# Attention kernel: the value matmuls of a step issued in one piece after the first couple of heads

## The chip, the cores and the metric

The kernel runs on one core of a Trainium2 chip. The metric is the device time of one execution in microseconds (us); lower is better. Its engines are named as in the profile: PE (TensorE matmuls), PEld (TensorE weight loads), DVE (VectorE), ACT (ScalarE), POOL (GpSimd), SP (SyncE, which issues the DMAs here).

## What is computed

The reference is one pre-norm transformer layer on x of shape (4, 2048, 256): x + attention(layernorm(x)), then + FFN(layernorm(x)). The attention is what matters here: 16 heads of width 16, rotary positions, causal, softmax in float32.

```
scores = einsum('bhqd,bhkd->bhqk', Q, K) / sqrt(16)
scores = where(causal_mask, -inf, scores)
attn = softmax(scores);  out = einsum('bhqk,bhkd->bhqd', attn, V)
x = x + einsum('bsd,ed->bse', out, Wo)
x = x + relu(layernorm(x) @ w1 + b1) @ w2 + b2
```

## The kernel before, in words

Three stages follow each other: `stage1` (layernorm, projections, rotation), `stage2` (attention, the largest) and `stage3` (output projection and FFN). The change touches `stage2` alone.

`stage2` runs 16 iterations, one for each batch entry and group of four heads (G = 4). An iteration has 40 steps (`STEPS`, NS = 40). A step is a pair (c, kb): c is one of four chunks of 512 queries, kb a block of 128 keys. A chunk c has 4c full steps (kb under 4c), then four diagonal steps, whose scores are 512, 384, 256 and 128 columns wide. An iteration thus has 24 full and 16 diagonal steps.

Two computations are interleaved:

- Scores, exponentials and values of step s. `score_tile` (L829) makes, for each head j = 0 to 3, a tile of 128 keys by up to 512 queries in PSUM. The four tiles of a step go round three banks (`SB = 3`, `s_bank`), and a tile waits (`p_done`, `read_before`) until ACT has read the tile three before it in the order of all tiles. ACT takes the exponential of each tile (L960) into `prob`, of which there are three buffers; POOL zeroes the triangle in diagonal steps (L990). `pv_step` (L848) multiplies the values with `prob` of step s - 2 (`BEHIND` = 2), for four heads on four strips of 32 columns of the array, accumulating in one bank (`O_BANK`) over the chunk. It is issued in two parts, each with half of the columns of all four heads. Only part 0 waits (for `p_done` or `mask_done`, and at a chunk's start for `o_copied`); part 1 counts `pv_done`, for which ACT waits before it writes a `prob` buffer again and before it copies the finished chunk (L951).
- Row maxima, 20 steps ahead (`LAG`). `max_pair` (L191, with small masking matmuls at L196 in couple 0 of diagonal tiles) makes query-by-key scores of a couple of heads into two banks. There are four such banks: couple 0 (heads 0/1) has two, couple 1 (heads 2/3) the other two. Before each matmul PE waits (`m_read`) until DVE has read what was in its bank. DVE takes the maximum of a couple with one reduce (L208), except that couple 1 of a diagonal tile takes two masked operations (L215), each of which waits for one matmul only. After a chunk's last tile three small DVE operations (L907, L912, L917) pass the maxima on.

The order on PE is written out by hand in `iteration` of `stage2`'s tensor block. In all steps that have maxima it is, for each couple: score, max, score, max, then a half of the value step:

```
for pair in range(NP):
    score_tile(i, p, s, 2 * pair)
    max_pair(nc, pe, ops, ps, t, pair, (1,))
    score_tile(i, p, s, 2 * pair + 1)
    max_pair(nc, pe, ops, ps, t, pair, (0,))
    value_step(i, p, s, pair)
```

The last 20 steps of the last iteration have no maxima (t reaches `STEPS_M`). They take another order, with two value parts, and the last two value steps are called after the loop, also with two parts. PE carries out its queue in order: a matmul that waits holds all behind it. On DVE and ACT it is the same.

Of the kernel before, what the change touches and what calls it, by code (L numbers as in the profile page):

```python
# [28 lines left out]
CH = 512  # L29
NC = S // CH  # L30
TPC = CH // P
# [19 lines left out]
NS = len(STEPS)  # L51
# [11 lines left out]
def is_diagonal(s):  # L63
    c, kb = STEPS[s]
    return kb >= TPC * c


def diagonals(s):

    return sum(is_diagonal(t) for t in range(s))  # L70
# [91 lines left out]
def m_use(t, j):  # L162

    return G * t + j
# [15 lines left out]
def max_pair(nc, pe, ops, ps, t, pair, heads=(1, 0)):  # L180

    p, use = t // NS % 2, m_use(t, 2 * pair)
    if pair == 0 and t % NS == 0:
        pe.wait_ge(ops.m_in[p], 128 * (t // NS // 2 + 1))
    qt, kc = MAX_TILES[t % NS]
    w = min(CH, (qt + 1) * P - kc * CH)
    for jj in heads:
        rows = slice(HROWS * jj, HROWS * (jj + 1))
        pe.wait_ge(ops.m_read, use + 2 - jj)
        masked = masked_on_pe(pair, qt, kc)  # L190
        last = nc.tensor.matmul(ps[:, bank_of(use + jj), 0:w], ops.mq[rows, p, pair, qt * P:(qt + 1) * P],  # L191
                                ops.mk[rows, p, pair, kc * CH:kc * CH + w], start=True, stop=not masked)
        for part in range(2 if masked else 0):

            n = P - HROWS * part
            last = nc.tensor.matmul(ps[:, bank_of(use + jj), w - n:w], ops.pick[rows, part], ops.upper[rows, part, 0:n],  # L196
                                    start=False, stop=part == 1)
        last.then_inc(ops.m_ready, 1)
# [456 lines left out]
def stage2(nc, x, qk_d, v_d, att_d, rows_d, rinv_d, weight_ds, weights, ops):  # L655
    with ExitStack() as ctx:
# [6 lines left out]
        part, m_ready, m_read = ops.part, ops.m_ready, ops.m_read  # L663
# [31 lines left out]
        BEHIND = NPROB - 1  # L695
# [9 lines left out]
        def s_bank(s, j):  # L705

            return S_BANK + (G * s + j) % SB

        def read_before(i, s, j):

            u = G * s + j
            last_in_bank = u - SB if u >= SB else max(t for t in range(ST) if t % SB == u) - ST
            return ST * i + last_in_bank + 1

        def prob_of(i, s):
            return prob[:, (NS * i + s) % NPROB]
# [96 lines left out]
        @block.tensor  # L813
        def _(pe):
            def filler_pair(p, s, pair):

                qt, kc = MAX_TILES[(s + LAG) % NS]
                for jj in range(2):
                    rows = slice(HROWS * jj, HROWS * (jj + 1))
                    nc.tensor.matmul(ps[:, M_BANK + 2 * pair + jj], mq[rows, p, pair, qt * P:(qt + 1) * P],  # L820
                                     mk[rows, p, pair, 0:CH], start=True, stop=True)

            def score_tile(i, p, s, j):

                c, kb = STEPS[s]
                q0 = max(0, kb - TPC * c) * P
                pe.wait_ge(p_done, G + read_before(i, s, j))
                rows = slice(HROWS * (j % 2), HROWS * (j % 2 + 1))
                nc.tensor.matmul(ps[:, s_bank(s, j), q0:CH], ak[rows, p, j // 2, kb * P:(kb + 1) * P],  # L829
                                 aq[rows, p, j // 2, c * CH + q0:(c + 1) * CH], start=True, stop=True  # L830
                                 ).then_inc(s_ready, 1)

            def pv_step(i, p, s, part):

                c, kb = STEPS[s]
                q0 = max(0, kb - TPC * c) * P
                half = (CH - q0) // 2
                if part == 0:
                    if kb == 0:
                        pe.wait_ge(o_copied, NC * i + c)  # L840
                    if is_diagonal(s):
                        pe.wait_ge(mask_done, G * (NDIAG * i + diagonals(s) + 1))
                    else:
                        pe.wait_ge(p_done, ST * i + G * s + G + G)
                cols = slice(q0 + half * part, q0 + half * (part + 1))
                for j in range(G):

                    last = nc.tensor.matmul(ps[32 * j:32 * j + 32, O_BANK, cols], v[:, p, kb, j, :],  # L848
                                            prob_of(i, s)[:, j, cols], start=kb == 0 and part == 0,
                                            stop=kb == TPC * (c + 1) - 1 and part == 1)  # L850
                if part == 1:
                    last.then_inc(pv_done, 1)

            def value_step(i, p, s, part):

                if s >= BEHIND:
                    pv_step(i, p, s - BEHIND, part)
                elif i > 0:
                    pv_step(i - 1, 1 - p, NS + s - BEHIND, part)

            def iteration(i, p, use):

                pe.wait_ge(a_in[p], A_DMAS * 16 * (use + 1))
                pe.wait_ge(v_in[p], 16 * (use + 1))
                for s in range(NS):
                    t = NS * i + s + LAG
                    if t == STEPS_M:
                        pe.wait_ge(m_read, NM + m_use(STEPS_M, 0))
                    if s in CHUNK_START:
                        pe.wait_ge(rows_in[STEPS[s][0]], 16 * ROWS_DMAS * (i + 1))  # L870
                    if t < STEPS_M:


                        for pair in range(NP):
                            score_tile(i, p, s, 2 * pair)
                            max_pair(nc, pe, ops, ps, t, pair, (1,))
                            score_tile(i, p, s, 2 * pair + 1)
                            max_pair(nc, pe, ops, ps, t, pair, (0,))
                            value_step(i, p, s, pair)
                        continue  # L880
                    score_tile(i, p, s, 0)
                    score_tile(i, p, s, 1)
                    if is_diagonal(s):
                        filler_pair(p, s, 0)
                    score_tile(i, p, s, 2)
                    value_step(i, p, s, 0)
                    score_tile(i, p, s, 3)
                    if is_diagonal(s):
                        filler_pair(p, s, 1)
                    value_step(i, p, s, 1)  # L890

            for t in range(EARLY, LAG):
                for pair in range(NP):
                    max_pair(nc, pe, ops, ps, t, pair)
            for u in range(NIT // 2):
                iteration(2 * u, 0, u)
                iteration(2 * u + 1, 1, u)
            for s in range(NS - BEHIND, NS):
                for part in range(2):
                    pv_step(NIT - 1, 1, s, part)  # L900
# [478 lines left out]
```

## Time and profile before

| | |
|---|---|
| median of 2 runs | 2064.44 us (2060.8 to 2068.07) |
| the profiled execution | 2068.45 us |
| its span | 2066.7 us |
| busy in the span: PE, DVE, ACT, POOL | 1958.2, 1835.6, 1515.4, 627.5 us |
| steps with scores and maxima | from 240 to 1589 us |

The profile's rows come from one execution. Times of a timeline are counted from the span's start; in its rows the first number is the start, the second the time to the end of the last of the instructions that the row merges. A PE matmul's end is modelled, and consecutive matmuls overlap, so PE's busy share says little of how full it is. For the same reason a DVE reduce or an ACT operation is reported a little longer than the distance at which the next one can start.

### The profile page before, as it was taken

The numbers are of one execution on the slowest core, as the hardware profiler recorded it, in microseconds if no ns is written. First come the engines' busy times: TensorE is split into PE (matmuls) and PEld (weight loads), VectorE is DVE, ScalarE is ACT, GpSimd is POOL, SyncE is SP. The second block draws the span as 40 slices with busy tenths as digits, with TensorE's granted clock in tenths as the row PEclk, the third lists the DMA queues.
The fourth block names the chain that finished last, engine by engine and source line by source line (L and its number), as shares of the span: only waits on it lengthen the run. The fifth ranks groups of instructions, "written<-read, shape, count | busy, mean of one in ns | idle before, by whom it ended". The sixth has DMA issues, their size and how long they took to land. (4 is left out here: it accounts for less than half of the span.)

```text
span 2066.7 us, 54533 instructions
## 1 busy us (share of the span) xinstructions
PE 1958.2 (95%) x20128; PEld 821.6 (40%) x20128; DVE 1835.6 (89%) x3190; ACT 1515.4 (73%) x3253; POOL 627.5 (30%) x1252
## 2 busy tenths in 40 slices
PE   6887799999999999999999999999999889999998
PEld 3444133232333333333333333333333156777776
DVE  7999999999999999999999999999997057777775
ACT  6995298887899888988889888898888623333332
POOL 8998022324221222212222122221212223333331
PEclk9998599999999999999999999999999689999999
DMA  5666533030312304123041230412301112222220
GB/s 206 229 241 216 113 74 69 18 70 18 80 38 55 70 18 80 37 56 70 18 80 36 57 69 19 80 34 58 69 8 35 55 64 86 86 85 81 84 84 26
DMA packets 133607, 153.49 MB, mean 74 GB/s; under 512 B 23936, under 2 KB 99712, under 8 KB 133120
## 3 DMA queue, kind: packets, MB, share of 16 engines
q1 hardware_dynamic: 133376, 150.46, 28.2%
q8 instruction: 140, 2.29, 0.5%
q14 instruction: 91, 0.75, 0.1%
HBM read 90.64 MB, written 59.77 MB: 73 GB/s over the span
## 5 line engine op out<-in xcount | busy, mean ns | idle before, releaser
L960 ACT ACTIVATE s_prob<-s_ps 128x512 f32<-128x512 f32 (+3 forms) x2560 | 1200.1, 536 | 159.8 <-PE s_ps L829 131.6
L208 DVE TENSOR_REDUCE part_max<-s_ps 128x2 f32<-128x1024 f32 (+3 forms) x1024 | 1082.7, 1117 | 13.6 <-PE s_ps L191 8.0
L829 PE MATMUL s_ps<-aq,ak 64*128 64x512 f16 (+3 forms) x2560 | 764.9, 355 | 4.4 <-ACT s_prob L960 1.7
L848 PE MATMUL s_ps<-s_prob,s_v 128*32 128x256 f32 (+3 forms) x10240 | 745.3, 363 | 0.0
L191 PE MATMUL s_ps<-mk,mq 64*128 64x512 f16 (+3 forms) x2560 | 654.0, 358 | 43.0 <-DVE part_max L208 34.9
L990 POOL TENSOR_SCALAR_AFFINE_SELECT s_prob<-s_prob 128x128 f32<-128x128 f32 x1024 | 292.1, 294 | 1105.6 <-ACT s_prob L960 1093.5
L829 PEld LDWEIGHTS s_ps<-aq,ak 64*128 64x128 f16 x2560 | 196.5, 94 | 478.2 <-ACT s_prob L960 413.2
L848 PEld LDWEIGHTS s_ps<-s_prob,s_v 128*32 128x32 f32 x10240 | 202.7, 108 | 392.1 <-issue 229.4
L215 DVE CUSTOM_DVE_ANT_0 s_ps<-s_ps,mask_sb 128x512 f32<-128x512 f32 (+3 forms) x512 | 241.4, 510 | 17.4 <-PE s_ps L191 16.9
L191 PEld LDWEIGHTS s_ps<-mk,mq 64*128 64x128 f16 x2560 | 156.5, 93 | 117.9 <-DVE part_max L208 98.5
L1263 ACT ACTIVATE s_h_f<-s_ps,s_b_s 128x512 f32<-128x512 f32 x128 | 88.0, 687 | 107.0 <-PE s_ps L1128 86.0
L1138 PE MATMUL s_ps<-w_hi,s_h_hi 128*128 128x256 f16 x512 | 139.6, 273 | 2.0 <-DVE s_h_lo L1203 2.0
L1138 PE MATMUL s_ps<-w_lo,s_h_hi 128*128 128x256 f16 x512 | 139.6, 273 | 0.0
L1138 PE MATMUL s_ps<-w_hi,s_h_lo 128*128 128x256 f16 x512 | 139.6, 273 | 0.0
L1203 DVE TENSOR_TENSOR s_h_lo<-s_h_f,s_h_hi 128x512 f16<-128x512 f32 x128 | 99.9, 781 | 4.4
L142 POOL TENSOR_TENSOR o_in<-o_in,r_in 128x1024 f32<-128x1024 f32 x16 | 37.8, 2365 | 189.5 <-DMA r_in<-rinv_scratch 189.5
L1201 DVE CAST s_h_hi<-s_h_f 128x512 f16<-128x512 f32 x128 | 61.8, 483 | 31.3 <-ACT s_h_f L1263 26.2
L196 PE MATMUL s_ps<-upper_sb,pick_sb 64*128 64x128 bf16 (+1 forms) x1024 | 89.1, 206 | 0.0
L1257 ACT CAST s_xt_hi<-s_ps 128x512 f16<-128x512 f32 x32 | 17.2, 589 | 89.8 <-PE s_ps L1118 89.8
L1128 PE MATMUL s_ps<-s_xt_hi,w_hi 128*128 128x512 f16 x256 | 77.4, 384 | 2.7 <-DVE s_xt_lo L1196 2.6
L1128 PE MATMUL s_ps<-s_xt_lo,w_hi 128*128 128x512 f16 x256 | 77.1, 383 | 0.0
L1128 PE MATMUL s_ps<-s_xt_hi,w_lo 128*128 128x512 f16 x256 | 77.1, 383 | 0.0
(103 smaller groups left out, 1772.9 us busy)
## 6 DMA issues: line engine op xcount, KB each, us to landing
v_scratch<-s_vst SPq DMA_DIRECT2D x32, 512.0 KB, 3.7
s_v<-v_scratch SPq DMA_DIRECT2D x16, 1024.0 KB, 12.2
att_scratch<-s_o SPq DMA_DIRECT2D x64, 256.0 KB, 2.5
aq<-qk_scratch SPq DMA_DIRECT2D x96, 128.0 KB, 4.4
ak<-qk_scratch SPq DMA_DIRECT2D x96, 128.0 KB, 7.2
s_xin<-x SPq DMA_DIRECT2D x16, 512.0 KB, 4.2
qk_scratch<-s_r_lo SPq DMA_DIRECT2D x64, 128.0 KB, 1.9
qk_scratch<-s_r_hi SPq DMA_DIRECT2D x64, 128.0 KB, 2.0
```

The source lines that it names most:

```text
L191: last = nc.tensor.matmul(ps[:, bank_of(use + jj), 0:w], ops.mq[rows, p, pair, qt * P:(qt + 1) * P], ops.mk[rows, p, pair, kc * CH:kc * CH ...
L196: last = nc.tensor.matmul(ps[:, bank_of(use + jj), w - n:w], ops.pick[rows, part], ops.upper[rows, part, 0:n], start=False, stop=part == 1)
L208: nc.vector.tensor_reduce(ops.part[:, qt // TPC, :, pair, qt % TPC, kc], ps[:, bank_of(use):bank_of(use) + 2, 0:w], AX.X, ALU.max).then_in ...
L215: nc.vector.tensor_tensor_reduce(out=ps[:, bank, 0:w], in0=ps[:, bank, 0:w], in1=ops.mask[:, CH - w:CH], scale=1.0, scalar=MASKED, op0=ALU ...
L829: nc.tensor.matmul(ps[:, s_bank(s, j), q0:CH], ak[rows, p, j // 2, kb * P:(kb + 1) * P], aq[rows, p, j // 2, c * CH + q0:(c + 1) * CH], st ...
L848: last = nc.tensor.matmul(ps[32 * j:32 * j + 32, O_BANK, cols], v[:, p, kb, j, :], prob_of(i, s)[:, j, cols], start=kb == 0 and part == 0, ...
L960: nc.scalar.activation(prob_of(i, s)[:, j, q0:CH], ps[:, s_bank(s, j), q0:CH], ACT.Exp, scale=1.0 / (SQK * DK ** 0.5)).then_inc(p_done, 1)
L990: nc.gpsimd.affine_select(out=block, in_=block, compare_op=ALU.is_ge, fill=0.0, base=0, pattern=[[1, P]], channel_multiplier=-1).then_inc( ...
L1128: last = nc.tensor.matmul(ps[:, H_BANK + f % 2], w[:, k, f * P:(f + 1) * P], a[:, p, k], start=q == 0, stop=q == len(mm) - 1)
L1138: last = nc.tensor.matmul(ps[:, Y_BANK + pair, t * D:(t + 1) * D], a[:, p, k, tt * P:(tt + 1) * P], w[:, k], start=q == 0, stop=q == len(m ...
L1203: nc.vector.tensor_tensor(h_lo[:, p, f], h_f[:, f % 2], h_hi[:, p, f], ALU.subtract).then_inc(hlo_done, 1)
L1263: nc.scalar.activation(h_f[:, f % 2], ps[:, H_BANK + f % 2], ACT.Relu, bias=b1_s[:, f:f + 1], scale=SH / SQK).then_inc(h_done, 1)
```

## The change

`pv_step` and `value_step` get a parameter `parts` (2 by default). In the steps that have maxima the value step is called once, after the maxima of couple 0, with `parts` = 1: four matmuls (one for each head) over all columns, which also count `pv_done`. Nothing stands after the maxima of couple 1, so that the scores and maxima of couple 1 are followed directly by those of couple 0 of the next step. The steps without maxima and the two last value steps stay as they were.

```diff
-            def pv_step(i, p, s, part):
+            def pv_step(i, p, s, part, parts=2):
...
-                cols = slice(q0 + half * part, q0 + half * (part + 1))
+                cols = slice(q0 + half * part, q0 + half * (part + 1)) if parts == 2 else slice(q0, CH)
                 for j in range(G):
 
                     last = nc.tensor.matmul(ps[32 * j:32 * j + 32, O_BANK, cols], v[:, p, kb, j, :],
                                             prob_of(i, s)[:, j, cols], start=kb == 0 and part == 0,
-                                            stop=kb == TPC * (c + 1) - 1 and part == 1)
-                if part == 1:
+                                            stop=kb == TPC * (c + 1) - 1 and part == parts - 1)
+                if part == parts - 1:
                     last.then_inc(pv_done, 1)
 
-            def value_step(i, p, s, part):
+            def value_step(i, p, s, part, parts=2):
 
                 if s >= BEHIND:
-                    pv_step(i, p, s - BEHIND, part)
+                    pv_step(i, p, s - BEHIND, part, parts)
                 elif i > 0:
-                    pv_step(i - 1, 1 - p, NS + s - BEHIND, part)
+                    pv_step(i - 1, 1 - p, NS + s - BEHIND, part, parts)
...
                             max_pair(nc, pe, ops, ps, t, pair, (0,))
-                            value_step(i, p, s, pair)
+                            if pair == 0:
+                                value_step(i, p, s, 0, 1)
```

## Rows read from the trace of the kernel before

**Rows 1.** The page: busy time, and granted clock by slices.

```profile
PE 1958.2 (95%) x20128; PEld 821.6 (40%) x20128; DVE 1835.6 (89%) x3190; ACT 1515.4 (73%) x3253; POOL 627.5 (30%) x1252
...
PEclk9998599999999999999999999999999689999999
```

**Rows 2.** What DVE waited for from 200 to 1600 us: total, times, longest.

```profile
DVE s_ps L215 <- PE s_ps L191: 16.9, 61, 0.7
DVE part_max L208 <- PE s_ps L191: 8.0, 20, 0.8
```

**Rows 3.** Timeline of a full step, in narrow windows.

```profile
1090.50 1.21 DVE L208 TENSOR_REDUCE part_max<-s_ps 128x2 f32<-128x1024 f32 x1
...
1090.64 0.57 PE L191 MATMUL s_ps<-mk,mq 64*128 64x512 f16 x2
...
1091.63 1.21 DVE L208 TENSOR_REDUCE part_max<-s_ps 128x2 f32<-128x1024 f32 x1
...
1091.77 0.57 PE L191 MATMUL s_ps<-mk,mq 64*128 64x512 f16 x2
1092.00 0.38 PE L829 MATMUL s_ps<-aq,ak 64*128 64x512 f16 x1
...
1092.31 0.42 PE L848 MATMUL s_ps<-s_prob,s_v 128*32 128x256 f32 x4
...
1092.88 0.39 PE L829 MATMUL s_ps<-aq,ak 64*128 64x512 f16 x1
...
1093.30 0.60 ACT L960 ACTIVATE s_prob<-s_ps 128x512 f32<-128x512 f32 x1
```

**Rows 4.** Timeline: a value part of 128 columns and the next score.

```profile
1037.47 0.43 PE L848 MATMUL s_ps<-s_prob,s_v 128*32 128x128 f32 x8
...
1037.83 0.39 PE L829 MATMUL s_ps<-aq,ak 64*128 64x512 f16 x1
```

**Rows 5.** Timeline: a reduce that waited for PE, and the maxima before it.

```profile
1053.73 0.60 PE L191 MATMUL s_ps<-mk,mq 64*128 64x512 f16 x2
...
1054.48 8.01 DVE L208 TENSOR_REDUCE part_max<-s_ps 128x2 f32<-128x1024 f32 x7 [0.38 <-PE s_ps L191]
```

**Rows 6.** Timeline in steps without maxima: exponentials, and weight loads of scores.

```profile
1600.18 3.54 ACT L960 ACTIVATE s_prob<-s_ps 128x512 f32<-128x512 f32 x7 [0.78 <-PE s_ps L829]
...
1600.83 0.09 PEld L829 LDWEIGHTS s_ps<-aq,ak 64*128 64x128 f16 x1 [0.44 <-ACT s_prob L960]
...
1601.81 0.09 PEld L829 LDWEIGHTS s_ps<-aq,ak 64*128 64x128 f16 x1 [0.21 <-ACT s_prob L960]
```

**Rows 7.** DVE's timeline through the diagonal steps of chunk 3.

```profile
1021.25 2.34 DVE L208 TENSOR_REDUCE part_max<-s_ps 128x2 f32<-128x1024 f32 x2
...
1023.51 0.69 DVE L215 CUSTOM_DVE_ANT_0 s_ps<-s_ps,mask_sb 128x512 f32<-128x512 f32 x1
...
1024.77 0.95 DVE L208 TENSOR_REDUCE part_max<-s_ps 128x2 f32<-128x768 f32 x1
1025.63 0.55 DVE L215 CUSTOM_DVE_ANT_0 s_ps<-s_ps,mask_sb 128x384 f32<-128x384 f32 x1
...
1026.62 0.68 DVE L208 TENSOR_REDUCE part_max<-s_ps 128x2 f32<-128x512 f32 x1
1027.28 0.43 DVE L215 CUSTOM_DVE_ANT_0 s_ps<-s_ps,mask_sb 128x256 f32<-128x256 f32 x1
...
1028.20 0.43 DVE L208 TENSOR_REDUCE part_max<-s_ps 128x2 f32<-128x256 f32 x1
1028.88 0.30 DVE L215 CUSTOM_DVE_ANT_0 s_ps<-s_ps,mask_sb 128x128 f32<-128x128 f32 x1 [0.26 <-PE s_ps L191]
...
1030.14 1.23 DVE L208 TENSOR_REDUCE part_max<-s_ps 128x2 f32<-128x1024 f32 x1
```

**Rows 8.** PE's timeline there: steps of 256 and of 128 columns.

```profile
1025.92 0.24 PE L196 MATMUL s_ps<-upper_sb,pick_sb 64*128 64x128 bf16 x2
1026.00 0.27 PE L829 MATMUL s_ps<-aq,ak 64*128 64x256 f16 x1
...
1026.20 0.64 PE L848 MATMUL s_ps<-s_prob,s_v 128*32 128x256 f32 x8
...
1028.44 0.28 PE L191 MATMUL s_ps<-mk,mq 64*128 64x128 f16 x2
```

## The prediction

> **What bounds the kernel now.** I read the page's shares first: PE 95% busy, DVE 89%, ACT 73% [rows 1]. PE's share is of modelled, overlapping ends, so the second view is a timeline of a full step [rows 3]. There the reduces stand 1.13 us apart (1090.50, 1091.63) with nothing between them. PE's max matmuls start 0.14 us after each (1090.64, 1091.77): they wait for the banks that the reduce just ended has read. A full step is two reduces, 2.26 us: DVE is the bound, and PE is held by it. The third view, what DVE waited for, says how little PE costs today: 16.9 + 8.0 us from 200 to 1600 us, mostly at the narrow masked tiles [rows 2]. So whatever the change saves on PE, no more than about 25 us (1.2%) can come back while the DVE work is unchanged. The question is whether the new order lets DVE starve.
>
> **What the parts of a step take.** I call V the time from the first value matmul to the next score. For 256 columns V is 0.57 us (1092.31 to 1092.88) [rows 3], for 128 it is 0.36 (1037.47 to 1037.83) [rows 4]. That is 0.21 for 128 columns more and 0.15 that is always there. For 512 columns in one piece this gives 0.36 + 3 x 0.21 = 0.99, I take 1.00. No row shows a piece of 512. The ends are 0.85 (only the 0.21 for each 128 columns, nothing fixed) and 1.14 (twice the half). I take 1.00, which is on the line through the two widths.
>
> **Removed.** One value-to-score turn per step: 2 x 0.57 - 1.00 = 0.14 us of PE's time, and the turn from scores to values, some 0.1 (couple 0 or 1 of score and max takes 0.54 from 1091.77 to the value part at 1092.31, of which two tiles of 512 columns stream at 0.23 each [rows 3]). About 0.24 us less PE work per full step. PE is held by DVE, so by itself this brings nothing. The value matmuls and weight loads are half as many and none waits longer: their wait still stands in front of the first part. `pv_done` comes earlier, so ACT's prob buffers and the copy of a chunk are freed earlier; no stall of weight was there, so I count 0. DMA and POOL work are the same. Cover for the later couple 1: the banks, examined next.
>
> **Moved: couple 1 now stands behind the whole value piece.** Two rings of waits lengthen.
>
> The score ring. Head 1 of the next step goes into the bank of head 2 of this step (three banks, four tiles). From the start of the head 2 score to its exponential is 0.42 us (1092.88 to 1093.30) [rows 3]. From the start of an exponential until PE may load the next tile of that bank is 0.65 (1600.18 to 1600.83) [rows 6]; two tiles on the same distance holds: exponentials stand 0.49 apart there ((3.54 - 0.60)/6, with 0.60 for one from rows 3), the third starts at 1601.16, and the load follows at 1601.81. From the head 1 score to the value piece is 0.31 (1092.00 to 1092.31) [rows 3]. Then V, then head 2. Sum: 0.42 + 0.65 + 0.31 + V. Before, the half of the value step after couple 0 (0.57) and the wait of head 1 shared a step of 2.26, and the ring was 1.38 + 0.57 = 1.95: slack 0.31. After: 1.38 + 1.00 = 2.38, over DVE's 2.26 by 0.12.
>
> The max ring. The start of a couple 0 reduce frees its banks for PE 1.13 + 0.14 = 1.27 later [rows 3]. Then 0.54 to the value piece [rows 3], V, and from the first max matmul of couple 1 to its reduce 0.75 (1053.73 to 1054.48, a reduce that waited for PE) [rows 5]. Then 1.13 for that reduce, after which couple 0's of two steps later can start. Sum over two steps: 3.69 + V; before 4.26 against DVE's 4 x 1.13 = 4.52; after 4.69, or 2.345 per step, 0.085 over the 2.26.
>
> The longer ring sets the pace: 2.38 against 2.26. With this pace DVE idles 0.12 us per step ahead of couple 1's reduce, and the max ring is satisfied too. ACT needs 4 x 0.49 = 1.96, so it keeps up.
>
> How many steps: the full steps whose value piece has 512 columns are those with kb of 2 or more, 2 + 6 + 10 = 18 in an iteration, 15 x 18 + 8 = 278 with the last one's first 20 steps. 278 x 0.12 = 33 us.
>
> The diagonal steps. I call their couple 0 reduce of the 512-wide tile 0. DVE's work then is 1.13, 1.26, 0.86, 0.99, 0.66, 0.73 for the operations up to the 128-wide tile (the starts 1023.51 to 1028.20, less the gap of 0.19 ahead of the last) [rows 7]. By the full step's pace the head 2 score starts at 0.50 (couple 1's reduce follows head 2 by 0.75 and couple 0's follows that by 1.13, the next head 2 comes 2.38 after the last: 2.38 - 0.75 - 1.13). The head 1 score of the next, 384-wide step starts 1.07 later at 1.57, the value piece 0.26 later, head 2 at 2.83. The masked operations wait for one max matmul: from its start 0.44 for 128 columns (1028.44 to 1028.88) [rows 7, 8], and I add 0.05 for each 128 columns more. So couple 1 of 384 starts at 3.38 where DVE could at 3.25, and ends at 4.37. For 256 columns: the exponential's turn is a little shorter (0.92 by my estimate, 1.07 less 0.15), head 1 at 3.75, the piece 0.20 later (1026.00 to 1026.20) [rows 8], V = 1.00, head 2 at 4.95, DVE at 5.45, where it could have started at 4.37 + 0.66 = 5.03: it idles 0.42. For 128: head 1 0.76 later at 5.71, piece at 5.86, of 384 columns (0.78), head 2 at 6.64, DVE at 7.08. It ends 0.64 later and takes 0.60 for the three small operations, so the next full reduce starts at 8.32. Before, that distance was 7.76 (1022.38, the second of the two merged reduces, to 1030.14) [rows 7]. So +0.56 for chunks 2 and 3. In chunk 1 no small operations follow: the same lay-out gives 7.76 where the distance was 7.49, +0.27. Chunk 0's first two pieces are only 256 and 128 wide: about +0.3. Together 1.69 an iteration, x 15 + 0.57 = 26 us.
>
> **Sum.** 33 + 26 = 59 us on the profiled execution's 2068.45, so 2127. That execution is 4 us over the median of the runs, 2064.44; against the median I predict 2123 us, 2.9% slower. A change of 2% is about what a measurement of this kernel can tell from none, some 41 us.
>
> The rule that speaks for the change: the fixed 0.15 us around each value part [rows 3, 4] is paid once less. The Trainium skill, "TensorEngine Tiling (Array Packing)", section Key Properties, says that a change of tiling mode drains TensorE; the values (four strips of columns) and the scores (two halves of the rows) are two modes, and the order of before changes them four times a step, the new one twice. By that rule alone PE gets faster, which is the first rival. The trace agrees as far as the fixed part goes (0.15 us beside 0.21 for 128 columns). A sum by the rule alone would be 0 to -25 us in place of +59; the rings are what speaks against it.
>
> **The rivals.** (1) PE's time counts, and the rings have the slack that I deny them: the turns saved let PE run ahead after each diagonal group, and DVE's 25 us of waits [rows 2] shrink. For it: the PE order was within a few hundredths of DVE's pace, and DVE waits for PE in every chunk. Against it: 0.12 us missing in the score ring. It decides if V(512) and the latencies sum to under 2.26, and gives 2064 - 25 = 2040 at best, 2050 likely. (2) One piece of 512 has no fixed part (V = 0.85): the score ring is 2.23, the max ring 2.27, full steps cost nothing, and the diagonal ones some 0.15 less for a wide piece, about 0.25 x 62 groups = 15 us: 2080. Against it: both widths seen have the fixed part. (3) One piece costs as much as two halves (1.14): the ring is 2.52, 278 x 0.26 = 72 us, the diagonal steps 26 + 62 x 0.14 = 35 us: 2171. To this I count that the granted clock falls where PE waits longer: it stands at full speed through the steps with maxima, and falls only where PE's work is thin (the fifth slice, and the end of the attention) [rows 1].
>
> **How the numbers follow.** Forecast (rings of 2.38, 2098 to 2150 by 0.05 us in the latencies on 278 + 62 places): 0.57, of which 0.05 lies within 2%. Rival 1: 0.15, of which 0.02 is faster by over 2%. Rival 2: 0.20. Rival 3: 0.08. So slower 0.52 + 0.08 = 0.60; same 0.13 + 0.20 + 0.05 = 0.38; faster 0.02. The range 2055 to 2155 leaves out most of rivals 1 and 3.
>
> **What would show it.** Right: reduces of couple 1 in full steps wait some 0.1 us for PE's max matmuls, the step is 2.35 to 2.40 us long, head 1's score load starts 0.65 after head 2's exponential, DVE's waits for L191 grow from 25 to 70 us or more, and value pieces stand 1.00 ahead of the next score. Wrong: reduces still 1.13 apart throughout; then look at V and at the distance from exponential to load. In the 256-wide steps DVE should idle about 0.4 us ahead of couple 1.

## The result, and the profile after

The changed kernel takes 2152.73 us (median of 2 runs, 2149.76 to 2155.7) against 2064.44: 1.043 of the time before, 95% interval 1.0373 to 1.0488. It is slower by 88 us, where the prediction had 59. Its profiled execution took 2155.70 us.

The page of the changed kernel, busy time and granted clock, answers to [rows 1]:

```profile
PE 1960.8 (91%) x15184; PEld 766.3 (36%) x15184; DVE 1859.7 (86%) x3190; ACT 1478.6 (69%) x3253; POOL 622.8 (29%) x1252
...
PEclk9997699999999999999999999999999689999999
```

PE has a quarter fewer matmul records, and all four engines have a smaller share of the span: no engine took the work over, all of them wait more. The clock's digits are nearly the same. What DVE waited for, from 200 to 1680 us (total, times, longest), answers to [rows 2]:

```profile
DVE s_ps L215 <- PE s_ps L191: 68.0, 151, 1.6
...
DVE part_max L208 <- PE s_ps L191: 7.4, 11, 1.6
```

The wait of L215, couple 1 of the diagonal tiles, grew from 16.9 to 68.0 us. That of L208 did not grow. The full steps' loss isn't in this view, as the view drops short gaps: there it is in the distances. The timeline of full steps of the changed kernel, against [rows 3]:

```profile
1139.77 13.18 DVE L208 TENSOR_REDUCE part_max<-s_ps 128x2 f32<-128x1024 f32 x11
...
1141.67 1.07 PE L848 MATMUL s_ps<-s_prob,s_v 128*32 128x512 f32 x8
...
1142.67 0.39 PE L829 MATMUL s_ps<-aq,ak 64*128 64x512 f16 x1
...
1143.09 2.06 ACT L961 ACTIVATE s_prob<-s_ps 128x512 f32<-128x512 f32 x4 [0.33 <-PE s_ps L829]
...
1143.74 0.09 PEld L829 LDWEIGHTS s_ps<-aq,ak 64*128 64x128 f16 x1 [0.22 <-ACT s_prob L961]
...
1144.07 1.06 PE L848 MATMUL s_ps<-s_prob,s_v 128*32 128x512 f32 x8
```

A value piece of four float32 matmuls, one for each head, stands in the trace as eight records (x8). The score ring can be read off link by link: value piece to head 2 score 1.00 us (1141.67 to 1142.67), to the exponential 0.42 (1143.09), to the weight load of head 1 of the next step 0.65 (1143.74), to the next value piece 0.33 (1144.07). That is 2.40; over the steps that follow the pieces stand 2.39 apart. The eleven reduces stand 1.196 us apart on average ((13.18 - 1.22) / 10) where they stood 1.13: two of them are the same 2.39. Single reduces, taken with narrow windows, show which of the two is late: couple 1's at 1143.42 starts 1.26 us after couple 0's, couple 0's follows couple 1's by 1.14.

```profile
1141.02 1.23 DVE L208 TENSOR_REDUCE part_max<-s_ps 128x2 f32<-128x1024 f32 x1
...
1142.16 1.22 DVE L208 TENSOR_REDUCE part_max<-s_ps 128x2 f32<-128x1024 f32 x1
...
1143.42 1.23 DVE L208 TENSOR_REDUCE part_max<-s_ps 128x2 f32<-128x1024 f32 x1
```

ACT waits 0.33 us ahead of every group of four exponentials, so it isn't the bound either.

DVE's timeline through the diagonal steps of chunk 3, against [rows 7]:

```profile
1132.81 29.71 DVE L208 TENSOR_REDUCE part_max<-s_ps 128x2 f32<-128x1024 f32 x25
...
1163.78 0.95 DVE L208 TENSOR_REDUCE part_max<-s_ps 128x2 f32<-128x768 f32 x1
1164.89 0.57 DVE L215 CUSTOM_DVE_ANT_0 s_ps<-s_ps,mask_sb 128x384 f32<-128x384 f32 x1 [0.15 <-PE s_ps L191]
...
1165.88 0.69 DVE L208 TENSOR_REDUCE part_max<-s_ps 128x2 f32<-128x512 f32 x1
1167.05 0.43 DVE L215 CUSTOM_DVE_ANT_0 s_ps<-s_ps,mask_sb 128x256 f32<-128x256 f32 x1 [0.48 <-PE s_ps L191]
...
1167.78 0.42 DVE L208 TENSOR_REDUCE part_max<-s_ps 128x2 f32<-128x256 f32 x1
1168.78 0.30 DVE L215 CUSTOM_DVE_ANT_0 s_ps<-s_ps,mask_sb 128x128 f32<-128x128 f32 x1 [0.58 <-PE s_ps L191]
...
1170.04 1.23 DVE L208 TENSOR_REDUCE part_max<-s_ps 128x2 f32<-128x1024 f32 x1
```

Ahead of each couple 1 DVE now stands idle, 0.15, 0.48 and 0.58 us, where before only the last had 0.26. From the 512-wide couple 0 reduce (the last of the 25, at 1132.81 + 29.71 - 1.22 = 1161.30) to the next full reduce it is 8.74 us against 7.76.

Laid side by side, one iteration in the middle of the attention (between two reciprocals of the softmax sums, L924 before and L925 after, one in each iteration but the first) takes 86.47 us before and 91.55 after, 5.08 more: the full stretches between diagonal groups grew by 0.29, 0.74 and 1.21 us (2.24), the diagonal groups of chunks 0 to 3 by 0.48, 0.66, 0.71 and 0.98 (2.83).

### The profile page after: what moved, and what is told of

Its sections match the earlier page's. It is cut to its first block and busy times, and to the rows that moved or that the text cites. A ratio compares the mean times of both kernels' runs of the same rounds, so it can differ in the third digit from the quotient of the medians.

```text
span 2154.0 us, 44645 instructions
## 1 busy us (share of the span) xinstructions
PE 1960.8 (91%) x15184; PEld 766.3 (36%) x15184; DVE 1859.7 (86%) x3190; ACT 1478.6 (69%) x3253; POOL 622.8 (29%) x1252
## 5 line engine op out<-in xcount | busy, mean ns | idle before, releaser
L961 ACT ACTIVATE s_prob<-s_ps 128x512 f32<-128x512 f32 (+3 forms) x2560 | 1171.8, 541 | 294.9 <-PE s_ps L829 287.7
L208 DVE TENSOR_REDUCE part_max<-s_ps 128x2 f32<-128x1024 f32 (+3 forms) x1024 | 1106.1, 1120 | 20.5 <-PE s_ps L191 7.4
L191 PE MATMUL s_ps<-mk,mq 64*128 64x512 f16 (+3 forms) x2560 | 701.3, 359 | 100.1 <-DVE part_max L208 93.7
L829 PE MATMUL s_ps<-aq,ak 64*128 64x512 f16 (+3 forms) x2560 | 703.3, 354 | 32.0 <-ACT s_prob L961 23.4
L991 POOL TENSOR_SCALAR_AFFINE_SELECT s_prob<-s_prob 128x128 f32<-128x128 f32 x1024 | 287.0, 292 | 1194.7 <-ACT s_prob L961 1177.9
L848 PE MATMUL s_ps<-s_prob,s_v 128*32 128x512 f32 (+3 forms) x5296 | 616.6, 539 | 0.0
L215 DVE CUSTOM_DVE_ANT_0 s_ps<-s_ps,mask_sb 128x512 f32<-128x512 f32 (+3 forms) x512 | 242.5, 512 | 69.8 <-PE s_ps L191 68.0
L191 PEld LDWEIGHTS s_ps<-mk,mq 64*128 64x128 f16 x2560 | 174.1, 94 | 323.1 <-DVE part_max L208 298.2
L848 PEld LDWEIGHTS s_ps<-s_prob,s_v 128*32 128x32 f32 x5296 | 105.4, 109 | 146.9 <-issue 98.2
L196 PE MATMUL s_ps<-upper_sb,pick_sb 64*128 64x128 bf16 (+1 forms) x1024 | 114.9, 206 | 0.0
L196 PEld LDWEIGHTS s_ps<-upper_sb,pick_sb 64*128 64x128 bf16 x1024 | 84.0, 96 | 21.5 <-issue 0.9
```

The source lines that it names most:

```text
L208: nc.vector.tensor_reduce(ops.part[:, qt // TPC, :, pair, qt % TPC, kc], ps[:, bank_of(use):bank_of(use) + 2, 0:w], AX.X, ALU.max).then_in ...
L215: nc.vector.tensor_tensor_reduce(out=ps[:, bank, 0:w], in0=ps[:, bank, 0:w], in1=ops.mask[:, CH - w:CH], scale=1.0, scalar=MASKED, op0=ALU ...
L961: nc.scalar.activation(prob_of(i, s)[:, j, q0:CH], ps[:, s_bank(s, j), q0:CH], ACT.Exp, scale=1.0 / (SQK * DK ** 0.5)).then_inc(p_done, 1)
L991: nc.gpsimd.affine_select(out=block, in_=block, compare_op=ALU.is_ge, fill=0.0, base=0, pattern=[[1, P]], channel_multiplier=-1).then_inc( ...
```

## The experiments

Each was run beside the kernel before on the same chip; times are medians. Theory: two rings of waits through the value piece, the score ring (three score banks) and the max ring (four max banks), set the pace as soon as they are longer than DVE's 2.26 us. The rivals were a cost in proportion to the piece's length, a cost of the late couple 1 alone, a cost of the single piece as such, and one ring only.

**e1, the piece after couple 1.**

```diff
-                            if pair == 0:
+                            if pair == 1:
                                 value_step(i, p, s, 0, 1)
```

> The value piece is still one piece, but stands after couple 1 instead of after couple 0. Ring theory (three score banks, four tiles): the piece now lies between the head 3 score and the head 0 score whose exponential frees head 3's bank: 0.31 + 1.00 + 0.48 + 0.65 = 2.44 us per full step with a wide piece, against 2.39 in the changed kernel and 2.26 before; the time is 2150 to 2175 us, 0 to 20 over the changed kernel. Rival (what costs is only that couple 1's maxima come late for DVE): with the piece behind couple 1 they come early again, and a good part of the 88 us comes back, 2064 to 2110 us.

Measured: 2157.02 us, ratio 1.0467 (1.0443 to 1.0492). Two views of it, waits of DVE and the timeline of full steps:

```profile
DVE part_max L208 <- PE s_ps L191: 67.6, 154, 1.7
DVE s_ps L215 <- PE s_ps L191: 0.3, 1, 0.3
```

```profile
1114.69 1.07 PE L848 MATMUL s_ps<-s_prob,s_v 128*32 128x512 f32 x8
...
1117.14 1.06 PE L848 MATMUL s_ps<-s_prob,s_v 128*32 128x512 f32 x8
```

The waits have changed place: couple 1 (L215) no longer waits, couple 0 (L208) waits for as much. The step is 2.45 us, 2.44 had been worked out. Neither of the two places is good for one wide piece; the rival falls.

**e2 and e3, the dose.** The first part gets three quarters (e2, shown) or seven eighths (e3) of the columns, in steps with maxima:

```diff
-                cols = slice(q0 + half * part, q0 + half * (part + 1))
+                cut = q0 + ((CH - q0) * 3 // 4 if use_cut else half)
+                cols = slice(q0, cut) if part == 0 else slice(cut, CH)
...
```

> Two parts as before the change, but three quarters of the columns after couple 0 and one quarter after couple 1 (V of 384 columns is 0.785, of 128 it is 0.36). Ring theory, which has a threshold: score ring 1.38 + 0.785 = 2.17, max ring (3.69 + 0.785) / 2 = 2.24, both under DVE's 2.26, so full steps cost nothing; the diagonal steps cost some 0.2 us a group, 12 us: 2064 to 2085 us, full steps at 2.26. Rival (a cost in proportion to how far the piece is lengthened): half of the 88 us, 2108.

> Seven eighths after couple 0, one eighth after couple 1 (V of 448 columns 0.89, of 64 0.25). Ring theory: score ring 2.27, max ring (3.69 + 0.89) / 2 = 2.29, 0.03 over DVE's 2.26: 8 us in the full steps, and some 0.45 us in each of the 62 diagonal groups, 28 us: 2100 us, 2085 to 2115. Rival (in proportion): three quarters of 88 us, 2130.

Measured: e2 2070.10 us, 1.0033 (1.0012 to 1.0055); e3 2092.22 us, 1.015 (1.0126 to 1.0174). The stretch of 25 reduces of 1024 columns ahead of the diagonal steps of chunk 3 in the kernel before, then in e2, then in e3, then value parts of e3:

```profile
1081.45 28.50 DVE L208 TENSOR_REDUCE part_max<-s_ps 128x2 f32<-128x1024 f32 x25
```

```profile
1086.91 28.50 DVE L208 TENSOR_REDUCE part_max<-s_ps 128x2 f32<-128x1024 f32 x25
```

```profile
1100.94 28.76 DVE L208 TENSOR_REDUCE part_max<-s_ps 128x2 f32<-128x1024 f32 x25
```

```profile
1111.88 0.96 PE L849 MATMUL s_ps<-s_prob,s_v 128*32 128x448 f32 x8
...
1114.17 0.96 PE L849 MATMUL s_ps<-s_prob,s_v 128*32 128x448 f32 x8
```

The same stretch takes 28.50 us in the kernel before, 28.50 with three quarters, 28.76 with seven eighths and 29.71 in the changed kernel. The dose has a threshold, where the rings put it, and e3's step is the 2.29 us of the max ring. In proportion e2 would have lost 44 us; it lost 8, nearly all of it at the diagonals. Both times lie in their expected ranges.

**e4, one piece only where it is narrow** (256 or 128 columns).

```diff
-                            if pair == 0:
-                                value_step(i, p, s, 0, 1)
+                            c, kb = STEPS[(s - BEHIND) % NS]
+                            if kb >= TPC * c + 2:
+                                if pair == 0:
+                                    value_step(i, p, s, 0, 1)
+                            else:
+                                value_step(i, p, s, pair)
```

> One piece after couple 0 only where the value piece is 256 or 128 columns wide (the last two diagonal blocks of a chunk), two halves elsewhere. Ring theory: V is at most 0.57 there, as long as half of a wide piece before the change, so no ring is over DVE's pace: no loss; the PE time saved (two turns in 8 of 40 steps) brings nothing, as DVE is the bound: 2058 to 2066 us. Rival (the single piece itself costs, whatever its length, by its single set of weight loads or by having nothing between couple 1 and the next couple 0): a fifth of the steps pay, some 10 to 18 us, 2075 to 2082.

Measured: 2053.85 us, 0.9958 (0.9941 to 0.9976). No loss: a single narrow piece costs nothing as such. That it was a little faster than all 16 runs of the kernel before beside it (2058.09 to 2070.26) was outside the expected range; e10 and e11 take that up.

**e5 to e8, shortening each ring.** e5 and e6 let L208 reduce only half of each bank outside the diagonal (`0:w // 2`), in the changed kernel and in the one before. e7 takes the exponential of half of the columns outside the diagonal (`q1 = CH // 2`), e8 does both; in these two the probabilities start from a memset. These kernels leave out work that the result needs, and serve to time the rings alone.

```diff
-                                ps[:, bank_of(use):bank_of(use) + 2, 0:w], AX.X, ALU.max)
+                                ps[:, bank_of(use):bank_of(use) + 2, 0:w if crosses_diagonal(qt, kc) else w // 2],
+                                AX.X, ALU.max)
...
+                        q1 = CH if is_diagonal(s) else CH // 2
-                        nc.scalar.activation(prob_of(i, s)[:, j, q0:CH], ps[:, s_bank(s, j), q0:CH], ACT.Exp,
+                        nc.scalar.activation(prob_of(i, s)[:, j, q0:q1], ps[:, s_bank(s, j), q0:q1], ACT.Exp,
```

> The changed kernel, but DVE's plain reduces (L208) outside the diagonal read only the first half of each bank, so that one takes about 0.60 instead of 1.13 us (the maxima are then those of half of the keys of these tiles). This takes DVE out of the full steps. Ring theory: the score ring (head 2 score, exponential, head 1 score of the next step, value piece) has no DVE in it and stays at 2.39 us per wide full step, so almost nothing is gained there: the time falls only in steps with narrow pieces and at the diagonals, 2153 to 2110 at most, value pieces still 2.39 apart. Rival (only the max ring or DVE's pace holds the changed kernel): the step falls to PE's own 0.54 + 1.00 + 0.43 = 1.97 us, 278 x 0.42 = 117 us less, about 2035.

> The same shorter reduces in the kernel before (the maxima are those of half of the keys of the full tiles). Both theories: DVE bounds it, so it gets faster until PE bounds it, at twice 0.54 + 0.57 = 2.22 us instead of 2.26 per full step, some 372 x 0.04 = 15 us less: 2050. With e5 it says whether the changed order needs more than DVE's pace.

> The changed kernel, but ACT takes the exponential of only the first 256 columns of each tile outside the diagonal (the others stay 0 or stale in the probabilities). The time from an exponential's start to the bank's release falls from 0.65 by about 0.22 us, so the score ring is 2.17; the max ring stays at 2.345. Ring theory: the pace of wide full steps becomes the max ring's, 2.34 to 2.36, so 278 x 0.04 = 11 us less, and little at the diagonals: 2135 to 2145. Rival (the score ring is the only one): the steps fall to DVE's 2.26, 36 us less, 2117.

> The changed kernel with both, the short exponentials and the short reduces of the full tiles. Both rings are then short (2.17 and 3.63 / 2 = 1.82), and a wide full step is the score ring's 2.17: 278 x 0.22 = 61 us less than the changed kernel, and some more in the steps with narrow pieces: 2070 to 2090. If neither ring holds the kernel, these cuts bring no more than e5 or e7 did.

Measured: e5 2092.09 us, 1.0134 (1.0077 to 1.0190); e6 2005.04, 0.9712 (0.9659 to 0.9765); e7 2126.68, 1.0301 (1.0242 to 1.0360); e8 2014.34, 0.9757 (0.9704 to 0.9810). Value pieces of two full steps in e5, each with the reduce ahead of it:

```profile
1167.90 0.69 DVE L208 TENSOR_REDUCE part_max<-s_ps 128x2 f32<-128x512 f32 x1 [1.00 <-PE s_ps L191]
...
1168.55 1.07 PE L849 MATMUL s_ps<-s_prob,s_v 128*32 128x512 f32 x8
...
1170.29 0.69 DVE L208 TENSOR_REDUCE part_max<-s_ps 128x2 f32<-128x512 f32 x1 [0.84 <-PE s_ps L191]
...
1170.94 1.06 PE L849 MATMUL s_ps<-s_prob,s_v 128*32 128x512 f32 x8
```

DVE idles 1.00 and 0.84 us ahead of these reduces, and the step is still 2.39 us. DVE's pace has nothing to do with it: this is the score ring alone, and the strongest single reading here. The fall of 61 us against the changed kernel was more than I had allowed (43). Of the 62.5 us between the two profiled executions 48.6 lie before the last reciprocal, most of them in steps where DVE was still the bound: those with narrow pieces, and the first ones, which have maxima alone. The other 13.9 lie behind it, where the clock of the changed kernel had halved and that of e5 hadn't (e10 and e11 look at this). With the same reduces the order of before takes 2005 us, so with a fast DVE the change costs 87 us as well. In e7, and then in e8 (the last row of e7 is cut off by its window):

```profile
1141.00 1.07 PE L848 MATMUL s_ps<-s_prob,s_v 128*32 128x512 f32 x8
...
1143.27 1.06 PE L848 MATMUL s_ps<-s_prob,s_v 128*32 128x512 f32 x8
...
1145.69 0.64 PE L848 MATMUL s_ps<-s_prob,s_v 128*32 128x512 f32 x4
```

```profile
1151.71 1.07 PE L849 MATMUL s_ps<-s_prob,s_v 128*32 128x512 f32 x8
...
1153.89 1.07 PE L849 MATMUL s_ps<-s_prob,s_v 128*32 128x512 f32 x8
...
1156.07 1.07 PE L849 MATMUL s_ps<-s_prob,s_v 128*32 128x512 f32 x8
```

With the exponentials short, two steps take 4.69 us, to the hundredth the max ring (3.69 + 1.00), unevenly split (2.27 and 2.42), as a ring that closes only after two steps allows. With both short it is 2.18, the shortened score ring. Each ring was made the pace in turn, at the length worked out for it. The totals of e7 and e8 missed their expected ranges, as they fell by more: e7 by 26 us, where 8 to 18 were expected, e8 by 138, where 63 to 83 were. In e7 the stretch from the first to the last reciprocal is 1282.0 us against 1293.8, the 11 us forecast, and the rest lies after it, in the last steps, where again only the changed kernel's clock had halved and where the short exponentials count too. In e8 that stretch is 1188.1 us, 106 less; the 0.21 us of 18 wide steps in each of its 14 iterations are 53 of them. The rest comes from the six full steps of an iteration with narrow pieces (kb 0 and 1), which together are 4.2 us shorter: I had put them at "some more".

**e9, the head 0 maxima ahead of the head 1 score** (for the diagonal steps, whose loss was under-counted).

```diff
                             max_pair(nc, pe, ops, ps, t, pair, (1,))
+                            if pair == 0:
+                                max_pair(nc, pe, ops, ps, t, pair, (0,))
                             score_tile(i, p, s, 2 * pair + 1)
-                            max_pair(nc, pe, ops, ps, t, pair, (0,))
+                            if pair == 1:
+                                max_pair(nc, pe, ops, ps, t, pair, (0,))
```

> The changed kernel with the max matmul of head 0, and the small masking matmuls after it, ahead of the head 1 score instead of behind it. In the changed kernel the head 1 score waits for its bank and holds them; in diagonal steps head 1 to value piece took 0.35, 0.30 and 0.24 us where I had counted 0.26, 0.20 and 0.15. If that is the term that the prediction had too small, it goes back to about the counted value: 0.3 us less in each of 62 diagonal groups, 15 to 19 us less than the changed kernel, 2134 to 2140, and full steps stay at 2.39 (the score ring has no max matmul in it). If the extra at the diagonals has another cause, the time stays at 2150 to 2157.

Measured: 2119.79 us, 1.0293 (1.0276 to 1.0310), 33 us less than the changed kernel and 14 below the expected range. Its reduces before the diagonal steps of chunk 3 and the one behind them, then value pieces of full steps:

```profile
1118.80 29.68 DVE L208 TENSOR_REDUCE part_max<-s_ps 128x2 f32<-128x1024 f32 x25
...
1155.61 1.22 DVE L208 TENSOR_REDUCE part_max<-s_ps 128x2 f32<-128x1024 f32 x1
```

```profile
1132.43 1.06 PE L848 MATMUL s_ps<-s_prob,s_v 128*32 128x512 f32 x8
...
1134.82 1.06 PE L848 MATMUL s_ps<-s_prob,s_v 128*32 128x512 f32 x8
```

The diagonal group of chunk 3 takes 8.35 us (1147.26 to 1155.61), where the changed kernel had 8.74 and the prediction 8.32; full steps stay at 2.39. From the first to the last reciprocal, with 14 of the iterations, it saves 16.3 us (1277.5 against 1293.8), 0.29 for each of 56 diagonal groups where 0.3 was expected. So the miss of the total lies elsewhere: the two profiled executions differ by 37 us, and beside these 16.3, 5.5 lie before the first reciprocal, not taken apart, and 15.3 after the last, where e10 and e11 look.

**e10 and e11, the last 20 steps.** `filler_pair` (two matmuls whose result nobody reads) in every one of them and not in diagonal ones alone, in e4's kernel and in the one before.

```diff
-                    if is_diagonal(s):
-                        filler_pair(p, s, 0)
+                    filler_pair(p, s, 0)
...
-                    if is_diagonal(s):
-                        filler_pair(p, s, 1)
+                    filler_pair(p, s, 1)
```

> The kernel of e4 (one piece only where it is 256 or 128 columns wide), and in the last 20 steps, which have no maxima, the filler matmuls stand in every step instead of only in diagonal ones. It is to tell what the 8 us of e4 are: in the profile before the granted clock fell to 0.52 and 0.59 there, in e4's to 0.89 and 1.00. If e4 gained by the clock of these steps alone, this one is not faster than the kernel before with the same fillers (e11), within 2 us, and both lie at 2050 to 2056. If the narrow pieces gain by themselves, it is 3 to 5 us faster than e11: 2048 to 2052.

> The kernel before with the filler matmuls in all of the last 20 steps. The clock stays up there: some 5 to 10 us less in executions where it fell, little in the others; 2052 to 2058, with a smaller spread than the kernel before.

Measured: e10 2057.82 us, 0.9982 (0.9969 to 0.9996); e11 2057.67 us, 0.9982 (0.9968 to 0.9996), both with 12 runs. Fifteen microseconds of the last steps in the kernel before, in the changed kernel, in e4 and in e11. Behind the window a row has its length and the busy time and instructions of PE, PEld, DVE, ACT and POOL, then the granted clock as a share of full speed, DMA share and GB/s:

```profile
1605.00:1620.00 15.00, 15.00 (x90) 2.76 (x89) 0.00 (x0) 9.83 (x19) 2.35 (x1) 0.52 0.30 114
```

```profile
1689.00:1704.00 15.00, 15.00 (x89) 2.69 (x88) 0.00 (x0) 9.17 (x18) 2.35 (x1) 0.50 0.30 115
```

```profile
1602.00:1617.00 15.00, 14.80 (x130) 3.99 (x129) 0.00 (x0) 12.77 (x26) 2.36 (x1) 0.89 0.31 115
```

```profile
1605.00:1620.00 15.00, 15.00 (x149) 3.90 (x146) 0.00 (x0) 12.47 (x25) 2.36 (x1) 1.00 0.30 113
```

e10 and e11 agree within 0.2 us, so with fillers in both the narrow pieces gain next to nothing (0.9 us between the first and the last reciprocal, 1216.9 against 1217.8). e10 came out 2 us above its expected range, e11 at the top of its own. Most of e4's 8 us were the clock of the last steps, which fell to half in the profiled execution before (0.52, with 19 exponentials in 15 us) and hardly did in e4's (0.89, with 26). Of the 11.3 us between these two executions 8.3 lie after the last reciprocal, 2.1 before the first and 0.9 between. The 23 runs of the kernel before beside e11 reach from 2056.58 to 2069.84, those of e11 from 2056.65 to 2059.41: the fillers take away the upper end and leave the lower one where it was. Only one of e4's nine runs has a trace; the mean granted clock of all nine is 0.977 to 0.980, against 0.969 to 0.977 for the kernel before beside it, and why it held in all of them isn't shown.

## Why the prediction was right, and what was too small

- **The bound, and what the change can gain.** Right: DVE's 2.26 us step was the floor, and the PE time saved brought nothing. e4, which saves PE two turns in 8 of 40 steps, gained 0.9 us by it between the first and the last reciprocal, and e10 against e11 as little. e6 shows the floor from the other side: with shorter reduces the kernel before goes to 2005 us. I had expected 2050. The wide full steps fell to 2.21 us, by the little that I had counted (2.22); of the 63 us between the profiled executions 51 lie before the last reciprocal, most of them in the steps with narrow pieces and in the first ones with maxima alone, whose floor I had left out, and 12 behind it, where the clock of the last steps held.
- **V of a 512-wide piece.** Taken at 1.00 by a line through two widths; measured 1.00. The ends 0.85 and 1.14 (rivals 2 and 3) fall with it.
- **The score ring.** Links 0.42, 0.65, 0.31 and 1.00, all found as counted (0.33 for the third). 2.38 became 2.39; e5 isolates it at this length, e8 at its shortened one.
- **The max ring.** 2.345; e7 isolates it at 4.69 for two steps, e3 at 2.29.
- **Full steps.** 33 us predicted. 2.24 us in an iteration were measured against 18 x 0.12 = 2.16; over the 15.4 iterations that 278 such steps make, it is 34 us.
- **Diagonal steps.** This is the term that was mis-sized: 1.69 us in an iteration, measured 2.83, so 44 us in place of 26 over 15.5 iterations. What was too small is the distance from the head 1 score to the value piece. I had taken it from [rows 8] (0.20 for 256 columns), where head 1 isn't held and some of the masking matmuls come ahead of it. In the changed kernel head 1 waits for its bank and holds the head 0 max and its two masks behind it. The timeline of PE in the diagonal steps of chunk 3, changed kernel:

```profile
1162.98 0.33 PE L829 MATMUL s_ps<-aq,ak 64*128 64x384 f16 x1
...
1163.33 1.06 PE L848 MATMUL s_ps<-s_prob,s_v 128*32 128x512 f32 x8
...
1165.25 0.28 PE L829 MATMUL s_ps<-aq,ak 64*128 64x256 f16 x1
...
1165.54 1.06 PE L848 MATMUL s_ps<-s_prob,s_v 128*32 128x512 f32 x8
...
1167.30 0.23 PE L829 MATMUL s_ps<-aq,ak 64*128 64x128 f16 x1 [0.22 <-ACT s_prob L961]
...
1167.54 0.85 PE L848 MATMUL s_ps<-s_prob,s_v 128*32 128x384 f32 x8
```

  The three distances are 0.35, 0.29 and 0.24 us, some 0.1 more each than counted, and the first head 2 score also comes 0.1 later (0.60 us after the couple 0 reduce that starts at 1161.30, where I had 0.50); their sum is the missing 0.4 of the group (8.74 against 8.32). e9 takes the masks out from behind head 1, and the group falls to 8.35. It does so in every chunk: the groups of chunks 0 to 3 cost 0.18, 0.39, 0.15 and 0.42 us more than predicted, and e9 gives back 0.09, 0.38, 0.18 and 0.39 of it (means over eleven iterations; in chunk 1 the full step behind the group is counted in).
- **What is left.** 34 + 44 = 78 of the 87 us between the two profiled executions. The two differ by 7.5 us up to the first reciprocal, 75.9 between the first and the last, 3.9 after it. Of the 14 iterations between them twelve grew by 5.0 to 5.5 us, 5.23 on average, so the one with 5.08 that I took apart was a mild one. The first and the last grew by 6.54 and 6.66, and in these two stretches the granted clock of the changed kernel was lower (0.96 and 0.98) than before the change (0.98 and 1.00). Of the 3.9, 0.3 lie before the last reduce, 1.3 in the steps without maxima and 2.2 in `stage3`, which I didn't take apart.
- **The range.** The measured 2152.73 lies 2 us inside the stated 2055 to 2155 and outside the narrower 2098 to 2150 that I gave to the rings themselves; one of the two runs took 2155.70. That narrower range was also wrongly worked out: 0.05 us at 278 + 62 places is 17 us, so 2106 to 2140. With the diagonal steps 18 us too small, it is partly luck that the time stayed inside. The mechanism doesn't hang on it, as the links and e5 to e9 show.
- **The mode rule.** A single piece does save PE the fixed part once: 1.00 us for 512 columns against twice 0.57. That said nothing of the time, since PE wasn't the bound. What the fixed 0.15 us consists of, the change of mode or the weight loads of the piece, no run separates.
- **The signs named.** Step 2.35 to 2.40: yes. About 0.4 us idle ahead of couple 1 in the 256-wide step: 0.48. DVE's waits for L191 over 70 us: 75. Reduces of couple 1 in full steps some 0.1 us late: yes, by their distance (1.26 against 1.14), though the view of waits doesn't list gaps this short.

## What to carry to other kernels

An engine that carries out its queue in order closes rings with those that feed and empty its banks: for each bank add up the way from its being written, through its reader, back to the next write, with everything that stands in the queue between them, and compare the sum with the bound engine's pace. In this kernel a longer block cost nothing in the full steps while the longest ring stayed under that pace (e2), and the whole surplus in every step from there on (e3 and the change itself); the total of the engine's work didn't show it. When an instruction starts to wait, what is queued right behind it is no longer spread out: count it behind the wait.

## What the runs showed that I had not expected

The granted clock in the last 20 steps, which have no maxima, differs between executions of one kernel. From the last reduce to the last exponential the profiled execution of the kernel before took 54.6 us, at 0.52 to 0.59 over 35 of them; e11, whose fillers keep PE fuller, took 45.5 us at full clock. The kernel before reaches from 2056.6 to 2069.8 us; with filler matmuls in each of those steps the spread is 3 to 4 us. The profiled executions of the kernel before and of the changed one both had the low clock there (0.52 and 0.50), so their difference of 87 us is hardly touched by it. Comparisons of 1% between variants of this kernel need it in view: e4 looked 0.4% faster mostly by it, and e5, e7, e8 and e9, whose traces kept the clock, look up to some 12 us faster against the changed kernel than their order or their cuts made them.
